# Two narrow score tiles in one half-array visit, and an experts' first product with its operands exchanged

## The reference

```python
def _L0_ffn_ref(x, centroids, gamma, beta, W1, b1, W2, b2):      # E = 8 experts, 128 -> 512 -> 128
    expert = jnp.argmax(feats @ centroids.T, axis=1)             # one expert per row
    alpha = sigmoid(sum(feats * centroids[expert]))
    # of the chosen expert e:
    h = normalized(feats) * gamma[e] + beta[e]
    y = feats + relu(h @ W1[e].T + b1[e]) @ W2[e].T + b2[e]
    return alpha * y + (1 - alpha) * feats

def _L0_attn_b_ref(x, Wq, Wk, Wv, Wo, bo):                       # 16 heads of 64
    q, k, v = split_heads(x @ Wq), split_heads(x @ Wk), split_heads(x @ Wv)
    q, k = apply_rope(q), apply_rope(k)                          # pairs (x1, x2) -> (x1 cos - x2 sin, x1 sin + x2 cos)
    sim = einsum(q, k) * scale, masked to the causal triangle
    return softmax(sim) @ v, heads joined, @ Wo + bo
```

## Time and profile before

| | |
|---|---|
| median of 3 runs | 4546.34 us (4544.78 to 4546.63) |
| profiled execution | 4553.04 us, span 4551.3 us |
| granted TensorE clock, mean | 0.914 |
| PE busy | 3865.9 us (85%) |
| VectorE busy | 2942.4 us (65%) |
| ACT busy | 2199.5 us (48%) |
| GpSimd busy | 2037.1 us (45%) |

### The profile page before, as it was taken

How to read it: one execution, slowest core, us unless ns; L and a number is a source line. 1 busy time by engine, 2 the same in 40 slices (tenths; PEclk the granted TensorE clock), 3 DMA queues, 4 the chain that set the end, 5 groups by cost and what they waited for, 6 DMA issues and landing times. The chain is left out here.

```text
span 4551.3 us, 88432 instructions
## 1 busy us (share of the span) xinstructions
PE 3865.9 (85%) x30129; PEld 2339.5 (51%) x30129; DVE 2942.4 (65%) x6716; ACT 2199.5 (48%) x5502; POOL 2037.1 (45%) x2133
## 2 busy tenths in 40 slices
PE   6999999846969999999999999967857767787668
PEld 2333333235736565565655656545646655586445
DVE  6888888664456666666666666554456657735477
ACT  2676666732335555555555555532355533423334
POOL 2222222155445665556655666554311116705278
PEclk9999999957979999999999999967979988978879
DMA  4433433121231111111111111122322220200000
GB/s 92 62 59 56 62 57 57 25 83 56 63 83 43 38 44 41 42 43 38 45 41 42 43 38 43 33 86 58 85 54 64 68 49 7 55 26 1 1 5 38
DMA packets 400926, 219.37 MB, mean 48 GB/s; under 512 B 247634, under 2 KB 343298, under 8 KB 399330
## 3 DMA queue, kind: packets, MB, share of 16 engines
q1 hardware_dynamic: 383188, 195.39, 19.5%
q0 software_dynamic: 8640, 17.97, 1.2%
q10 hardware_dynamic: 8656, 0.35, 0.1%
HBM read 79.79 MB, written 41.50 MB: 27 GB/s over the span
## 5 line engine op out<-in xcount | busy, mean ns | idle before, releaser
L2412 POOL TENSOR_TENSOR ra_prob<-ra_prob,ra_inverse 128x256 f32<-128x256 f32 (+3 forms) x512 | 642.2, 1254 | 672.1 <-DVE ra_inverse L2594 495.6
L2561 ACT ACTIVATE ra_prob<-ra_ps_s,ra_low 128x128 f32<-128x128 f32 (+3 forms) x1024 | 532.7, 528 | 750.0 <-DVE ra_low L2586 750.0
L2236 DVE TENSOR_REDUCE ca_mx<-ca_ps_s 128x2 f32<-128x1024 f32 x512 | 600.5, 1210 | 112.2 <-PE ca_ps_s L2097 111.8
L2586 DVE TENSOR_REDUCE ra_low<-ra_ps_s 128x2 f32<-128x256 f32 (+3 forms) x512 | 419.4, 819 | 369.8 <-PE ra_ps_s L2490 190.0
L2162 ACT ACTIVATE ca_pT<-ca_ps_p 128x512 f32<-128x512 f32 x1024 | 547.7, 601 | 220.7 <-PE ca_ps_p L2107 218.7
L2436 PE MATMUL ra_ps_t<-ident,ra_prob 128*128 128x128 f32 x2560 | 404.8, 282 | 31.5 <-ACT ra_probT L2544 25.5
L2097 PE MATMUL ca_ps_s<-ca_kst,ca_qst 128*128 128x512 bf16 x1024 | 395.6, 392 | 37.5 <-DVE ca_mx L2236 21.0
L2107 PE MATMUL ca_ps_p<-ca_qst,ca_kst 128*128 128x512 bf16 x1024 | 386.2, 382 | 4.0 <-ACT ca_pT L2162 3.9
L2436 PEld LDWEIGHTS ra_ps_t<-ident,ra_prob 128*128 128x128 f32 x2560 | 269.4, 141 | 160.6 <-issue 98.3
L2506 PE MATMUL ra_ps_o<-ra_probT,ra_v 128*64 128x512 f32 (+3 forms) x2048 | 332.4, 445 | 0.0
L2405 POOL TENSOR_TENSOR ra_rot<-ra_prod 128x512 f32<-128x512 f32 x256 | 320.2, 1273 | 11.9 <-DVE ra_prod L2580 11.9
(11 more groups left out here) (427 smaller groups left out, 7823.1 us busy)
## 6 DMA issues: line engine op xcount, KB each, us to landing
ra_qz<-ra_rot SPq DMA_DIRECT2D x512, 64.0 KB, 2.0
ra_kz<-ra_rot SPq DMA_DIRECT2D x512, 64.0 KB, 2.0
ca_kst<-ca_bounce SPq DMA_DIRECT2D x256, 64.0 KB
ca_bounce<-ca_thirds SPq DMA_DIRECT2D x192, 64.0 KB, 3.0
ca_qst<-ca_bounce SPq DMA_DIRECT2D x64, 192.0 KB
moe_hs<-moe_rows SPq DMA_DIRECT2D x142, 66.0 KB
moe_raw<-in_L_ffn_W SPq DMA_DIRECT2D x32, 256.0 KB
moe_hx<-moe_back SPq DMA_DIRECT2D x16, 512.0 KB, 7.0
```

Source lines behind the costliest of these rows:

```text
L2236: nc.vector.tensor_reduce(mx[:, hm % 2, 2 * j:2 * j + 2], ps_s[m % 2][:].rearrange("p (b k) -> p b k", b=2), AX.X, ALU.max)\
L2412: nc.gpsimd.tensor_tensor(at, at, inverse[:, n % PROB, 2 * tile:2 * tile + 2].unsqueeze(2).broadcast_to([P, 2, keys]), ALU.mult)\
L2561: nc.scalar.activation(prob[:, score % PROB, t, head, 0:keys], ps_s[u % 2][:, head * 512:head * 512 + keys], ACT.Exp, bias=low[:, score % ...
L2586: nc.vector.tensor_reduce(low[:, score % PROB, 2 * t:2 * t + 2], ps_s[u % 2][:].rearrange("p (h k) -> p h k", h=2)[:, :, 0:keys], AX.X, AL ...
```

## The change

Experts: the first product takes 128 columns of the expert's weights as stationary operand and the transposed rows as moving one, four times, so that the result comes out with the hidden unit in the partition and the row in the column. The four transposes per block and the bank for them go. [...] The bias becomes one number per partition and group of 128 columns (`b1T`); it is made by 32 columns of products in one bank, without the wide beta, and b1 is no longer broadcast.

Rope attention: slot t = 0 now computes the scores of tiles 0 and 1, both on half the rows per head, with the masks first; slot t = 1 computes none. VectorE takes both minima in slot 0, and ACT's exponentials of tile 0 wait for both. `qz` loses its zero half and its memset. On ACT the copy of head 1's transposes goes ahead of the output copy.

```diff
@@ expert_ffn
-        b12 = sb("b12", [P, E, H + D])
+        b1_rows, b1T, b2_wide = sb("b1_rows", [E * HC, P]), sb("b1T", [P, E, HC]), sb("b2_wide", [P, E, D])
-        beta_wide = sb("beta_wide", [P, E, P])
+        w1_own = sb("w1_own", [P, OWN, H])
...
+                sp.dma_start(b1_rows[:], b1.rearrange("e (c f) -> (e c) f", f=P)).then_inc(sg["loaded"], 16)
-                        sp.dma_start(b12[:, :, 0:H], b1.partition_broadcast(P)).then_inc(sg["bias_loaded"], 16)
-                        sp.dma_start(b12[:, :, H:H + D], b2.partition_broadcast(P)).then_inc(sg["bias_loaded"], 16)
+                        sp.dma_start(b2_wide[:], b2.partition_broadcast(P)).then_inc(sg["bias_loaded"], 16)
...
                     sp.dma_start(hs[:, i % HS, :], rows[bass.ds(ats[i % 8], P), :]).then_inc(hs_in[i % HS], 16)
+                    wait(sp, sg["hidden"], i - OWN + 1)
+                    sp.dma_start(w1_own[:, i % OWN, :], w1T[:, bass.ds(own[i % 8], 1), :].rearrange("p a f -> p (a f)")).then_inc(own_in[i % OWN], 16)
...
+                nc.tensor.matmul(ps_b[:, 0:E * HC], b1_rows[:], core.ident[0:E * HC, 0:E * HC], start=True, stop=False, skip_group_check=True)
...
-                    pe.wait_ge(sg["beta_done"], e + 1)
-                    wait(pe, sg["b_done"], e)
-                    nc.tensor.matmul(ps_b[:], beta_wide[:, e, :], w1T[:, e, :], start=True, stop=True).then_inc(sg["b_in"], 1)
+                    for c in range(HC):
+                        last = nc.tensor.matmul(ps_b[:, e * HC + c:e * HC + c + 1], w1T[:, e, c * P:(c + 1) * P], cgb[:, 2, e:e + 1],
+                                                start=False, stop=(e == E - 1), skip_group_check=True)
...
                         pe.wait_ge(sg["hT_ready"], i + 1)
+                        pe.wait_ge(own_in[i % OWN], turn(i, OWN))
                         wait(pe, sg["act_done"], i - 1)
-                        nc.tensor.matmul(ps_h[i % 2][:], hT[:, i % 2, :], w1T[:, bass.ds(held[i], 1), :].rearrange("p a f -> p (a f)"), start=True, stop=True)\
-                            .then_inc(sg["hidden"], 1)
-                    if 0 <= s - 2 < NBLK:
-                        i = s - 2
-                        pe.wait_ge(sg["act_done"], i + 1)
-                        wait(pe, sg["actT_ready"], i - 1)
                         for c in range(HC):
-                            last = nc.tensor.transpose(ps_a[i % 2][:, c * P:(c + 1) * P], act[:, i % 2, c * P:(c + 1) * P], core.ident[:])
-                        last.then_inc(sg["a_turned"], 1)
+                            last = nc.tensor.matmul(ps_h[i % 2][:, c * P:(c + 1) * P], w1_own[:, i % OWN, c * P:(c + 1) * P],
+                                                    hT[:, i % 2, :], start=True, stop=True)
+                        last.then_inc(sg["hidden"], 1)
...
-                        act_e.wait_ge(sg["a_turned"], i + 1)
+                        act_e.wait_ge(sg["act_done"], i + 1)
-                        nc.scalar.activation(actT[:, i % 2].rearrange("p c t -> p (c t)"), ps_a[i % 2][:], ACT.Relu).then_inc(sg["actT_ready"], 1)
+                        nc.scalar.activation(actT[:, i % 2].rearrange("p c t -> p (c t)"), act[:, i % 2, :], ACT.Relu).then_inc(sg["actT_ready"], 1)
...
-                        bias = b12[:, bass.ds(held[i], 1), 0:H].rearrange("p a f -> p (a f)")
-                        nc.vector.tensor_tensor(act[:, i % 2, :], ps_h[i % 2][:], bias, ALU.add).then_inc(sg["act_done"], 1)
+                        bias = b1T[:, bass.ds(held[i], 1), :].rearrange("p a c -> p (a c)").unsqueeze(2).broadcast_to([P, HC, P])
+                        nc.vector.tensor_tensor(by_c(act[:, i % 2, :]), by_c(ps_h[i % 2][:]), bias, ALU.add).then_inc(sg["act_done"], 1)
@@ rope_attention
-        qz, kz = sb("qz", [P, RING, 2, S]), sb("kz", [P, RING, S])
+        qz, kz = sb("qz", [P, RING, S]), sb("kz", [P, RING, S])
+        VISITS = 3
+        visit = lambda n, t: VISITS * n + max(t - 1, 0)
+        part = lambda n, t: ps_s[visit(n, t) % 2][:].rearrange("p (h k) -> p h k", h=2)[:, :, P * (t == 1):P * (t == 1) + (t + 1) * P]
...
-                nc.gpsimd.memset(qz[:], 0.0).then_inc(prep, 1)
...
@@ PE, scores
+                    wait(pe, sg["exp_done"], 2 * (TC * n + {0: -1, 2: 0, 3: 2}[t]))
+                    bank = ps_s[visit(n, t) % 2]
+                    for head in range(2):
+                        if t == 0:
+                            diagonals = bank[:, head * 512:(head + 1) * 512].rearrange("p (two k) -> p two k", two=2)[:, :, 0:P]
+                            nc.tensor.matmul(diagonals, core.identb[:], mask[:].unsqueeze(1).broadcast_to([P, 2, P]), start=True, stop=False, skip_group_check=True)
+                        else:
+                            nc.tensor.matmul(part(n, t)[:, head, t * P:], core.identb[:], mask[:], start=True, stop=False, skip_group_check=True)
+                    for tile in (0, 1) if t == 0 else (t,):
+                        for head in range(2):
+                            half, keys = slice(head * DH, (head + 1) * DH), (tile + 1) * P
+                            last = nc.tensor.matmul(part(n, tile)[:, head, :], qz[half, n % RING, tile * P:keys], kz[half, n % RING, 0:keys],
+                                                    start=False, stop=True, skip_group_check=True)
...
-                    if score is not None:
+                    if score is not None and t != 1:
                         scores(t, score)
@@ ACT
+                    if value is not None:
+                        act.wait_ge(sg["p_turned"], 2 * (TC * value + t) + 2)
+                        wait(act, sg["pv_done"], TC * (value - 1) + t + 1)
+                        nc.scalar.copy(probT[:, 1, t, 0:S - t * P], ps_t[1][:, 0:S - t * P]).then_inc(sg["probT_act"], 1)
                     done = s - VALUE - 1
...
-                    if value is not None:
...
-                        act.wait_ge(sg["low_done"], u + 1)
+                        act.wait_ge(sg["low_done"], TC * score + max(t, 1) + 1)
@@ VectorE
-                    if score is not None:
+                    if score is not None and t != 1:
-                        dve.wait_ge(sg["s_in"], u + 1)
+                        dve.wait_ge(sg["s_in"], visit(score, t) + 1)
+                        for tile in (0, 1) if t == 0 else (t,):
+                            nc.vector.tensor_reduce(low[:, score % PROB, 2 * tile:2 * tile + 2], part(score, tile), AX.X, ALU.min).then_inc(sg["low_done"], 1)
```

69 lines of the change are left out of this document (24 added, 45 removed).

## The result

The changed kernel takes **4511.11 us** (4504.16 to 4518.25, 4 runs) beside 4545.56 us of the kernel before (4544.08 to 4546.63, 4 runs): ratio 0.9925, 95% interval 0.9907 to 0.9942. The forecast was 4501, range 4458 to 4545. The profiled execution took 4509.05 us (span 4507.1), 44.0 less than that of before, against a sum of -45. Both profiled executions of the changed kernel hold some 12 us of a stall that the prediction has no word for (runs 8 and 9).

A forecast was written before the change was run, and what follows sets the result against it. The prediction took PE as the bound by share in block loops and rope attention. Terms -60, +3, -10 and +22 sum to -45: 4508 us on the profiled execution, 4501 on the median's footing, range 4458 to 4545.

The forecast's parts named there:

- Sum: Whole kernel: block loops -60, copy at loop start +3, expert starts -10, rope +22, together -45 us.
- Block loops: Two expert layers, 71 blocks each: four transposes fewer on PE, period 2.30 to 1.87 us, -60 us.
- The copy: Expert weights, 262 KB per block on SP's queue: 1.08 us at 243 GB/s, hidden; +3 us at loop starts.
- Starts: Starts of the expert layers: smaller bias transfer removes VectorE's and PE's waits, -5 us per layer, -10 (0 to -13).
- ACT's order: Rope attention: copy of the probabilities put first on ACT ends 0.47 us sooner but gives nothing more.
- rival 2: Block loops: weights' copy becomes the bound through SP's ring and the 16 engines; total 4551 or 4589; chance 0.10.
- An earlier start comes through whole: Expert layers: POOL's scatters behind the start run gapless, so the -5 us per layer reaches the total.
- Rope, the visit: Rope attention: PE's merged score visit for tiles 0 and 1 takes 1.16 us, taken as 1.2, bounds 0.95 to 1.45.
- Rope, the chain: Third projection waits for VectorE's products: 5.15 us instead of 4.91; +0.28 per quad (four heads), rope stage +22.
- (1): Rope attention gains what PE is spared, -83 us instead of +22: total 4396; chance 0.08.
- (3): Rope attention: heads don't overlap or coupled waits cost more; visit 2.0 us, rope +120, total about 4600; chance 0.05.
- The signs: Loops: period near 1.87, DMA share near 0.8; rope quad: 25.6 to 25.9 us, PE busy 0.4 less, second-slot ACT wait gone.

The follow-up runs named there:

- run 8: Changed kernel with ACT's output copy ahead of the copy of the probabilities again, as before the change: 4504.99 us, ratio 0.9897.
- run 9: Changed kernel once more, with no edit: 4514.34 us, ratio 0.9925.
- run 11: Changed kernel with a second 262 KB copy of the weights for each block, into a ring nobody reads: 4560.54 us, ratio 1.0016.
- run 12: Changed kernel with the 2 MB broadcast of the first bias issued again, into a tile nobody reads: 4512.07 us, ratio 0.9915.
- run 3: Changed kernel with the scores of tiles 0 and 1 in two visits again, both on half rows: 4490.44 us, ratio 0.9861.
- run 4: Changed kernel with the four transposes between the second and third projection issued twice: 4515.42 us, ratio 0.9912.
- run 5: Changed kernel with two half-row visits again and ACT's output copy moved to the second slot: 4452.45 us, ratio 0.9782.
- run 6: Experts as changed, rope attention as in the kernel before except ACT's output copy in the second slot: 4462.55 us, ratio 0.9796.
- run 7: Changed kernel, merged visit kept, with ACT's output copy moved to the second slot: 4534.96 us, ratio 0.9966.

## Why the prediction was right, point by point

**Sum.** Forecast -45, profiled executions -44.0. By stage: block loops -47.3 (-57 with the copy's +3), starts up to the first scatter -12.1 (-10), rope +20.0 (+22), and three differences of which the prediction said nothing: scatters -6.2, the stall between scatters and blocks +12.5, the stages behind -8.9; smaller ones -2.2. That the two totals agree to 1 us is luck: the block loops missed by 10, and the other terms make that up. The three unforeseen terms nearly cancel in this pair of traces. In the medians it is -34.4. There the step failed that put the forecast on the median by taking 6.7 us off: the changed kernel's profiled execution lay below its median, not above. The kernel of run 8 has every term of the sum (ACT's order was put at nothing) and not the stall: ratio 0.9897 is -47 on 4551.6.

**Block loops.** The mechanism holds: 2.30 to 1.896, PE gapless in all but a few steps, clock 1.00, no wait for the weights' copy (over the first loop one of 0.9 us for rows). The size was off by 10: the period is 1.896, not 1.87 (17 passes of 0.11; the eight of the first product take 0.90 and not 0.87), 0.026 x 140 = 3.6; the loops of before were 159.3 and not 70 x 2.30 = 161, since they begin with a step of 0.44, which the new ones don't, 3.5; and start and register loads took 1.7 and 4.1 instead of 1.5 each, 2.8.

**The copy.** The row taken for its rate, 243 GB/s, was the wrong neighbour: same length of row and same memories, but 32 rows in a transfer instead of 128 (that this is why the rates differ no run shows). Measured 375 GB/s; forecast DMA share 0.83, measured 0.64. The Trainium skill (DMA: Bandwidth & Descriptors, Where 436 GB/s comes from) states 435 GB/s as the ceiling between SBUF and SBUF; the measured rate is 86% of it, so the page was nearer than the row. By it two copies fit into a block too, and the loops of run 11 are 53 us longer (324.3 against 271.3 of the changed kernel); that doesn't speak against the page, since SyncE's issues alone take longer than a block there. The prediction gave rival 2 two places, SyncE's ring and the engines, but priced only the engines; the issues, "about 0.4 us" each, are 0.34 and 0.49.

**Starts.** -5 a layer forecast, -5.4 and -6.7 measured, 4.3 and 3.5 of it by the transfer (run 12). The 64 passes with one column cost what the sum said, nothing: eight in 1.73 us (946.35 to 948.08) against 1.71 for the two of 512 columns. "An earlier start comes through whole" is the step that failed: in this program it did not, for the stall ahead of the blocks lost 6.9 and 4.7 us again. Nor were the scatters of the kernel before gapless, as that sentence had it: GpSimd pauses for 1.1 and 1.7 us in each layer.

**Rope, the visit.** 1.16 forecast, 1.17 measured. **Rope, the chain.** Third projection at 5.15 forecast, 5.14 measured; quad 25.75 and 25.75; before a new sequence 27.12 + 0.28 + 0.35 = 27.75 and 27.72. That this is cover lost and nothing else was argued from two timelines there; runs 3 and 4 show it. **ACT's order.** "It gives nothing more" holds (run 8). What the prediction did not see is that the same copy is worth 0.49 us a quad one slot later, if the visits are two (runs 5 to 7).

**The rivals.** (1) fell: the quad is longer, not shorter. (2) did not come about: the period is 1.896 and PE never waits for the copy. (3) fell with the visit of 1.17.

**The signs.** Three did not come as told. PE's busy time in a quad fell by 0.16 us and not by 0.4 or more, though by the cadence of starts the two visits are 0.74 shorter together (1.54 to 1.17 each). The DMA share of the loops was 0.64 and not near 0.8. And the wait for ACT's copy left the second slot (0.19 us), but one of 0.24 stands in the third, where VectorE's products are what the next projection waits for.

**What stays open.** What VectorE waits for in the stall (a stall of its own is 1.7 of the 3.5 us a layer that the scatters of the kernel before are longer than those of run 8); whether the DMA engines at 0.85 would hold PE back; what moves the unchanged stages by up to 15 us between kernels.

## What to carry to other kernels

Before merging two visits of an engine, ask what its work stood in front of: 0.60 us a quad saved on the busiest engine cost 0.37, because the work had covered another engine's chain between two uses of one bank. When a wait names a copy, look at what stands ahead of that copy on its engine; moving one copy by a slot gave 25 us, shortening the passes 4. For a transfer that must hide, find the price by doubling it, but count the issuing engine's time as well as the DMA engines': here three issues of 0.46 to 0.60 us and their gaps, 1.92 a block, were already longer than the block.
